# A four-stage transformer block with routed experts on one core: expert maps spread over the batches, loads and routed stage reordered

## The reference

```python
# 1 causal attention, 16 wide; the values are x itself
q = x @ w_q.T + b_q; k = x @ w_k.T + b_k
x = ln(x + softmax(mask(q @ k.T / 4)) @ x)
# 2 one linear map with ternary weights
x = ln(x + x @ (clip(round(w / s), -1, 1) * s).T)
# 3 q, k, v of x; a statistic of q and k per token, two small convolutions over the
#   tokens with a group norm (the ODE step), sigmoid, softmax over the 512 tokens;
#   v times that weight times a channel gate, then a projection
x = ln(x + (weights[..., None] * v * ch_w) @ proj_w + proj_b)
# 4 h = ln(x)*gamma+beta; a shared expert for all tokens and the best of 8 routed ones
out = silu(h @ sw1.T) @ sw2.T + p_top * (silu(h @ ew1[e].T) @ ew2[e].T)
x = ln(x + out)
```

## Time and profile before

| | us |
|---|---|
| median of 3 runs | 910.05 (909.46 to 910.09) |
| the profiled execution | 912.14 |
| its span, first to last instruction | 910.8 |
| TensorE busy | 782.4 (86%) |
| VectorE busy | 727.4 (80%) |
| ScalarE busy | 698.1 (77%) |
| GpSimd busy | 315.1 (35%) |

### The profile page before, as it was taken

One profiled execution on the slowest core, in us unless ns is written; L12 is line 12 of the kernel. 1 busy time (PEld: TensorE's weight loads), 2 busy tenths in 40 slices (PEclk: granted clock), 3 DMA queues, 4 the chain that ended last, 5 costly groups with the idle time before them and its releaser, 6 DMA issues. The chain is left out here.

```text
span 910.8 us, 18608 instructions
## 1 busy us (share of the span) xinstructions
PE 782.4 (86%) x5514; PEld 621.8 (68%) x5514; DVE 727.4 (80%) x2321; ACT 698.1 (77%) x1561; POOL 315.1 (35%) x384
## 2 busy tenths in 40 slices
PE   0568899999999999999999999988757878888783
PEld 0346678778878878878878877866435767767672
DVE  1777999778878878888887887977563889989995
ACT  0447887688697697697697797786746989999995
POOL 2000001012422323323333323434561555556556
PEclk9976999999999999999999999999887999999997
DMA  7132331110221211201203201101127775445441
GB/s 201 60 116 92 124 122 57 47 49 24 82 67 40 76 54 52 82 19 65 83 18 111 82 20 41 37 30 48 47 83 218 181 203 164 151 146 167 130 106 56
DMA packets 50979, 80.81 MB, mean 89 GB/s; under 512 B 8954, under 2 KB 27838, under 8 KB 50880
## 3 DMA queue, kind: packets, MB, share of 16 engines
q1 hardware_dynamic: 39056, 53.46, 20.7%
q0 software_dynamic: 9984, 25.29, 7.7%
q10 hardware_dynamic: 1840, 0.86, 0.3%
HBM read 49.57 MB, written 32.11 MB: 90 GB/s over the span
## 5 line engine op out<-in xcount | busy, mean ns | idle before, releaser
L3621 POOL DMA_INDIRECT out<-G_y,Gid x80 | 83.1, 1039 | 77.8 <-ACT G_y L1867 56.1
L1220 PE MATMUL bank<-E2T,G_Sh 128*128 (+1 forms) x320 | 74.3, 278 | 39.7 <-DVE G_Sl L3426 39.6
L3493 POOL DMA_INDIRECT rrec<-R,pos x64 | 64.3, 1005 | 82.0 <-DVE R L2111 67.2
L1849 ACT ACTIVATE G_S<-bank,e1b,e1s 128x256 f32<-128x256 f32 x160 | 91.6, 693 | 0.0
L519 PE MATMUL bank<-X,PT 128*128 128x257 f32 x320 | 82.5, 392 | 2.5 <-DVE X L1954 1.3
L3484 POOL DMA_INDIRECT hrec<-HN,pos x64 | 65.3, 1020 | 52.0 <-DVE pos L2234 37.2
L3452 POOL TENSOR_TENSOR R<-rstd,mhalf 128x4 f32<-128x4 f32 x16 | 17.4, 1089 | 184.2 <-DVE rstd L1910 184.2
L1208 PE MATMUL bank<-G_T,E1T 128*128 128x256 f16 x640 | 80.0, 280 | 1.0 <-DVE G_T L3417 1.0
L3460 POOL TENSOR_TENSOR R<-V,mhalf 128x8 f32<-128x8 f32 x16 | 26.7, 1666 | 142.7 <-DVE V L1920 142.7
L1220 PE MATMUL bank<-E2T,G_Sl 128*128 (+1 forms) x320 | 74.6, 278 | 0.0
L1208 PEld LDWEIGHTS bank<-G_T,E1T 128*128 (+1 forms) x640 | 64.4, 101 | 9.7 <-issue 1.4
(11 more groups left out here) (362 smaller groups left out, 2597.5 us busy)
## 6 DMA issues: line engine op xcount, KB each, us to landing
G_r<-rrec SPq DMA_DIRECT2D x40, 258.0 KB
G_h<-hrec SPq DMA_DIRECT2D x40, 257.0 KB, 2.8
X<-in_x SPq DMA_DIRECT2D x16, 512.0 KB, 5.2
XT<-in_xT SPq DMA_DIRECT2D x16, 512.0 KB, 4.3
e1n<-in_ew SPq DMA_DIRECT2D x8, 512.0 KB, 3.4
e2n<-in_ew SPq DMA_DIRECT2D x8, 512.0 KB, 3.4
rrec<-rpad SPq DMA_DIRECT2D x18, 129.0 KB, 4.9
hrec<-hpad SPq DMA_DIRECT2D x18, 128.5 KB, 4.7
```

What stands on the lines that cost most here:

```text
L1220: last = pe.matmul(banks[j][:, 0:D], x[w % NGB][:, f, j * P:(j + 1) * P], E2T[:, expert_of[w], f, :], start=k == 0, stop=k == 2 * FC - 1)
L1849: act.activation(G_S[w % 2][:, ff, :], bk[:, (ff - f0) * SLOT:(ff - f0 + 1) * SLOT], ACT.Silu, bias=e1b[:, expert_of[w], ff], scale=e1s[:, ...
L3493: pool.indirect_dma_start(rrec[:], bass.IndirectOffsetOnAxis(pos[b % 2][:, j:j + 1], 0), R[b % 2][:, j, :], None).then_inc(s[f"rrec{b % 2} ...
L3621: pool.indirect_dma_start(t["out"], bass.IndirectOffsetOnAxis(Gid[w % 6][:, j:j + 1], 0), G_y[w % 3][:, j, :], None, bounds_check=TOK - 1, ...
```

## The change

Shared and routed maps: the shared expert's map and the first routed one are made in the opening; the other seven come one per pair (`one0`, `one1`, `one_et0` and their like, map g+2 in pair g), in bank 2, between two ODE steps. The map buffers move: e1n, e2n and the clipped parts now share one place. `dg` is gone: `map_dg` multiplies a broadcast scale with the identity. `guard` runs twice, once for the shared expert, once for the routed ones, with a scale each. `rank` uses bank 6 in place of bank 2, and `up(b, 1)` waits for `place(b, 0)` in place of the first router step.

```diff
+        def load_e1(q):
+            if q == 1:
+                sp.wait_ge(s["et0"], 1)
+            elif q >= 2:
+                sp.wait_ge(s["et1"], q)
+                sp.wait_ge(s["dgm"], q)
+        def load_e2(q):
             if q >= 1:
+                sp.wait_ge(s["et0"], q + 1)
...
             pe.wait_ge(s["m0"], 7 * q + 5)
-            if q >= 1:
-                pe.wait_ge(s["e2s"], q)
-            b16 = banks[6][:].bitcast(F16)
+            if q == 1:
+                pe.wait_ge(s["e2s"], 1)
+            elif q >= 2:
+                pe.wait_ge(s["ode"], NO * (q - 1))
+            b16 = banks[6 if q < 2 else 2][:].bitcast(F16)
...
             if g >= 1:
-                pe.wait_ge(s["place"], at("place", GB * g - 1, 0))
+                pe.wait_ge(s["e2s"], g + 2)
...
             elif f == 1:
-                pe.wait_ge(s["rout"], at("rout", b, 0))
+                pe.wait_ge(s["place"], at("place", b, 0))
```

```diff
+        load_xT(0)
+        load_e1(0)
+        load_x(0)
+        load_e2(0)
+        load_xT(1)
+        load_small()
+        load_x(1)
+        load_e1(1)
+        load_tiny()
+        load_e2(1)
```

```diff
-            pe.matmul(bk[:, 0:w], KH[:, t], Qs[:, k * P:SEQ], start=True, stop=False)
-            pe.matmul(bk[:, 0:w], KL[:, t], Qs[:, k * P:SEQ], start=False, stop=False)
+            pe.matmul(bk[:, 0:w], Ks[:, t], Qs[:, k * P:SEQ], start=True, stop=False)
...
+            act.activation(Qs[64:128, :], banks[0][0:64, :], ACT.Identity, bias=bqk[0:64, :]).then_inc(s["qkhi"], 1)
```

```diff
-NGR, NGB = 4, 3
+NGR, NGB, NGS, NGY, NGI = 5, 4, 3, 4, 8
...
-            act.activation(G_Sh[w % NGB][:, f0:f0 + 2], G_S[w % 2][:, f0:f0 + 2], ACT.Copy, scale=sdn[:]).then_inc(s["gSh"], 1)
+            act.activation(G_Sh[w % NGB][:], G_S[w % NGS][:], ACT.Copy, scale=sdn[:, 1:2]).then_inc(s["gSh"], 1)
...
+            if j == 0:
+                if w < NF:
+                    expert_of[w] = bass.DynSlice(dve.value_load(q_exi[0:1, w:w + 1], min_val=0, max_val=NE - 1), 1)
...
-            dve.scalar_tensor_tensor(G_y[w % 3][:, j, :], banks[j][:, 0:D], G_r[w % NGR][:, j, D:D + 1], G_e2[w % 4],
+            dve.scalar_tensor_tensor(G_y[w % NGY][:, j, :], banks[j][:, 0:D], G_r[w % NGR][:, j, D:D + 1],
+                                     e2s[:, expert_of[w], :].rearrange("p o d -> p (o d)"),
```

More of the change, by code:

```diff
@@ L253, in program @@
     front_end = here[0]
-    here[0] = late_end
+    here[0] = front
     q_n = sb("q_n", [P, NE])
@@ L871, in pe_program @@
+        for i in range(4):
+            pv(1, i)
+        x2T(0, 0)
+        map_et1(1)
+        map_dg(1)
         x2T(0, 1)
-        map_dg(3)
         proj(2)
@@ L1115, in pe_program @@
-        rank(12)
+        hT(13, 0)
+        hT(13, 1)
+        guard_max(1)
+        for i in range(1, 4):
+            u(14, i)
+        logits(13)
         x2T(15, 0)
-        down(12, 0)
+        up(13, 0)
+        guard_bound(1)
+        rank(13)
         x2T(15, 1)
-        down(12, 1)
-        down(12, 2)
+        up(13, 1)
+        up(13, 2)
+        one_dg(7)
         gate1(15)
         dqk(15, 0)
-        down(12, 3)
         gate2(15)
-        dqk(15, 1)
-        hT(13, 0)
-        hT(13, 1)
@@ new lines, in act_program @@
+        gexp(1)
+        PS_(1)
+        one_r0(0)
+        x1c(2, 0)
+        Mh_(1)
+        for i in range(1, 4):
+            x1c(2, i)
+        qk(3)
+        T1h_(2, 0)
+        U_(1, 0)
+        U_(1, 1)
+        T1h_(2, 1)
+        U_(1, 2)
+        nmr_(3)
+        oexp(0)
+        U_(1, 3)
+        sq2(2, 0)
+        oexp2(0)
+        exp(3, 0)
+        sq2(2, 1)
+        exp(3, 1)
+        exp(3, 2)
+        sq2(2, 2)
+        exp(3, 3)
+        sq2(2, 3)
+        for i in range(4):
+            sq3(0, i)
@@ new lines, in dve_program @@
+        x2(1, 0)
+        chw(0, 3)
+        qklo(2)
+        qks(0, 3)
+        x2(1, 1)
+        x2(1, 2)
+        Ml_(0)
+        x2(1, 3)
+        max_(2, 0)
+        map0(1, 5)
+        ve0(1)
+        ve1(1)
+        max_(2, 1)
+        max_(2, 2)
+        guard(0, 0)
+        max_(2, 3)
+        x2p(0, 2)
+        map0(1, 6)
+        guard(0, 1)
+        one0(0, 0)
+        TTl_(1, 0)
+        one0(0, 1)
+        guard(0, 2)
+        TTl_(1, 1)
+        one0(0, 2)
+        rinv(2, 0)
+        x2p(0, 3)
@@ new lines, in dve_program @@
+        x2p(1, 0)
+        x1(2, 0)
+        rinv(2, 1)
+        x1(2, 1)
+        x2p(1, 1)
+        guard(0, 3)
+        qks(1, 0)
+        chw(1, 0)
+        bn0(2, 0)
+        chw(1, 1)
+        chw(1, 2)
+        rinv(2, 2)
+        chw(1, 3)
+        x1(2, 2)
+        bn0(2, 1)
+        qks(1, 1)
+        qks(1, 2)
+        one0(0, 3)
+        bn0(2, 2)
+        qks(1, 3)
+        guard(0, 4)
+        for i in range(3):
+            ode(0, i)
+        mv_(2, 0)
+        ode(0, 3)
+        ode(0, 4)
@@ new lines, in dve_program @@
+        ode(0, 18)
+        ode(0, 19)
+        max_(3, 3)
+        x2(2, 0)
+        guard(0, 7)
+        ode(0, 20)
+        ode(0, 21)
+        x2(2, 1)
+        ode(0, 22)
+        one0(0, 6)
+        ode(0, 23)
+        ode(0, 24)
+        x2(2, 2)
+        ode(0, 25)
+        ode(0, 26)
+        x3(0, 0)
+        x2(2, 3)
+        x3(0, 1)
+        x3(0, 2)
+        ve1(2)
+        rinv(3, 0)
+        x3(0, 3)
+        x1(3, 0)
+        guard(0, 8)
+        rinv(3, 1)
+        x2p(1, 3)
+        ve2(0)
@@ L3224, in dve_program @@
-        router(12, 6)
-        place(12, 0)
-        TTl_(15, 1)
-        x2p(15, 0)
-        ve2(13)
-        r(12, 0)
-        y(12, 1)
-        y(12, 2)
+        acc(12)
+        HTl_(13, 0)
+        HTl_(13, 1)
+        guard(1, 1)
+        guard(1, 2)
+        for i in range(3):
+            router(13, i)
+        rg(12)
+        for i in range(3, 6):
+            router(13, i)
+        TTl_(15, 0)
+        guard(1, 3)
+        place(13, 0)
+        x2p(15, 0)
+        Sl_(13, 0)
+        TTl_(15, 1)
```

2759 lines of the change are left out of this document (1284 added, 1475 removed), and 2 rows, old and new, of the table names.

## The result

The changed kernel takes **896.9 us** (median of 4 runs, 893.8 to 897.4) against 909.8 for the kernel before (909.2 to 910.1): ratio 0.985 [0.983, 0.988]. It is 12.9 us faster where 37 were forecast, and outside the range. Its profiled execution took 893.8 us (span 892.4), the fastest of its four, 18.3 less than the profiled one of before (912.1, span 910.8).

What follows compares the result with a forecast made beforehand. The prediction took TensorE's work to bound the loop over pairs, a dependent chain the drain, and mainly ScalarE the routed stage. Terms -12 - 8 + 5 - 8.5 + 1.5 - 15 = -37 gave 873 us, range 855 to 893.

Steps and rivals of the forecast that it cites:

- Load order, -12: Opening: issuing XT, X and the shared maps first starts attention earlier; -12 us, bounds -5 and -18.
- Maps leave the opening, -8: 44.6 to 157 us: seven maps fewer relieve VectorE and cut TensorE's idle and half-clock time; -8 us, bounds +3 and -20.
- One product, -8.5: Loop: transposed scores lose their second product, 0.60 us in each of some 14 batches; -8.5 us, bounds -7 and -10.
- Routed stage, -15: Routed stage: period falls from 5.11 to 4.70 us over 39 steps, fill +1; -15 us, bounds -3 and -19.
- Rival B: Routed stage keeps its period because VectorE is close behind ScalarE; -15 becomes -3, 885 us; chance 0.11.
- The drain, +1.5: Drain after the loop: later `up(b,1)`, eighth map and second guard cost little; +1.5 us, bounds -5 and +6.
- The same maps in the loop, +5: Loop: added VectorE and ScalarE work stays under TensorE, only waiting in order costs; +5 us, bounds 0 and +20.
- the loop's TensorE idle passes 20 us: Loop: sign that would show the prediction wrong, TensorE idle above 20 us.
- TensorE above 98% in the loop: Loop: sign expected if the maps term holds, TensorE busy above 98% beside VectorE at 90%.
- A: Loop slows: with VectorE at 91%, in-order queues leave TensorE waiting, +12 to +16 us; 887 us; chance 0.17.
- C: Loop: the map's chain stalls TensorE in every pair; slower from 5.3 us per map, 922 us at 7; chance 0.06.
- D: After the opening: the half-clock stretch vanishes, -10 us more; 863 us; chance 0.06.

Runs made afterwards that it cites:

- e8: e3 with the first XT, X and the shared expert's two tables loaded ahead of the small weights; 886.9 us.
- e3: The kernel before with two parts of the change, transposed scores as one product and the new routed stage, its front's order and maps untouched; 897.0 us.
- e12: e8 with VectorE's first list put in the order in which the loads land, all maps still in the opening; 883.7 us.
- e15: e13 with every piece of a map moved a few places later in the loop's lists; 899.4 us.
- e1: The kernel before with only the transposed scores as one product, including the third pass of q this needs; 904.1 us.
- e2: The kernel before with only the changed kernel's routed stage; 898.8 us.
- e9: The changed kernel with the loop's seven maps left out whole (set to zero at the start), the order of all else kept; 899.5 us.
- e13: e12 with seven maps moved from the opening into the loop, one per pair, the loop's lists otherwise in the old order; 930.7 us.
- e4: The changed kernel with the product of the transposed scores issued twice; 904.6 us.
- e5: The changed kernel with the loop maps' VectorE and ScalarE work cut to 16 columns for seven experts, TensorE transposing a constant; 936.4 us.
- e6: The changed kernel with only VectorE's work on the seven loop maps cut to 16 columns, TensorE transposing a constant; 926.5 us.

## Why the prediction was wrong, step by step

**Load order, -12: right, the exact figure in part by luck.** e8 shows 12.1, but its opening ran at a mean granted clock of 0.81 up to the projection of batch 4 and e3's at 0.88, so the two don't differ by the loads alone. In the changed kernel the first projection came at 7.83 (forecast 9) and the first reciprocal at 29.54 (32). On the way there VectorE's opening went otherwise than I had it:

```profile
14.29 1.22 DVE L2336 TENSOR_REDUCE esc<-e2n 128x2 f32<-128x1024 f32 x1 [1.33 <-DMA e2n<-in_sw]
...
17.17 0.69 DVE L2314 TENSOR_SCALAR e1n<-e1n 128x1024 f32<-128x1024 f32 x1 [1.59 <-ACT e1n L1461]
...
18.69 0.74 DVE L1942 SCALAR_TENSOR_TENSOR Qs<-bank,bqk,Qs 32x512 fp32r<-32x512 f32 x1
```

The second shared map was there at 14.3, not 19, since the first 20 us moved 265 GB/s and not 200. The Trainium skill's rule on queues taking turns (DMA: Bandwidth & Descriptors, "Queues, rings and completion order") is neither confirmed nor refuted: what VectorE needed from both queues had landed before the split of q and k could tell, and that split stood at 18.69 behind ScalarE's rounding.

**Maps leave the opening, -8: right in kind, too small.** e12 and e15 have the same loads first and differ in where the maps are: their projections of batch 4 stand 12.9 us apart (151.6 and 138.8), so -12.9, 1.8 us per map. The mean granted clock up to there is 0.85 and 0.84, so this comparison is an even one.

**One product, -8.5: the size was off, and -5.0 lies outside its bounds of -7 and -10.** e1's interval is -6.5 to -2.6. I multiplied the distance between two starts by the columns, 1.2 us per pair; the step became 1.0 shorter and its neighbours took part of that back, so the pair gained 0.68.

**Routed stage, -15: right.** -15.6 in the stage here, -14.2 in e2 (whose median moved by 10.3 only). The period is 4.71, with ScalarE at 174.6 and VectorE at 173.2 of 183.7, so both, not VectorE alone as I wrote, are nearly full. Rival B is refuted.

**The drain, +1.5: within its bounds.** The stretch from projection 14 to the first `gy` became 3.5 us shorter where 0 were forecast. It also holds one pair, so the drain by itself has no figure.

**The same maps in the loop, +5 (bounds 0 and +20): this is the step that failed.** The pair cost 5.9 us per pair against e1, about 33 over the loop. The step said: "Both stay under TensorE, so their work is covered; what is not covered is waiting in order", and behind it stood "only work taken off TensorE shortens it". I priced the waiting that the new order brings at 0.8 us per pair, from two places that I had looked at, and took the maps' own work on TensorE, 1.4 us per pair, as the same in the opening and in the loop. By e9 the order is the large part: without the maps the pair stays at 75.0.

Of the 5.9 us some 2.8 are idle time of TensorE (15.7 of 416 us in the loop) and 1.4 its own work on a map. The remaining 1.7 are spread over steps that take longer from start to start though no idle time stands in them: the block-3 statistics of q and k 12.3 for 11.6 us per pair, the transposes of `HN` 1.9 for 1.5, block 3's `u` 3.4 for 3.1. That this is waiting too is suggested, not shown, by the weight loads: per pair they are busy 54.8 us in e1 (190.8 / 240 x 69.0) and 56.2 after (180.3 / 240 x 74.8), longer by no more than the maps' own work. By that, some 4.5 of the 5.9 us are waiting, against the 0.8 of the step. In e9 the same sum is about 3 of idle time, no map work, about 1 for the clock and 2 for the longer steps: that its pair equals the changed kernel's is in part a coincidence, and does not show that the maps cost nothing there.

This agrees with a rule of the Trainium skill (Perfetto Trace Analysis, section "Identifying the Most-Contended Engine") that I did not weigh: the matmuls' busy share is a bad measure of how full TensorE is, and the weight loads' share a better one. It was 80% before, not 99.8. I had taken that a kernel whose TensorE is busy 99.8% of a stretch has slack everywhere else. It has none in its *order*: in the old one the view names no wait of TensorE in these 240 us, in the new one some come in every pair, though no engine's load explains it.

My sign for it, "the loop's TensorE idle passes 20 us", was a bad one: idle in 157 to 578 is 17.1 us, so it just didn't ring, at a loss of 28. The other one, "TensorE above 98% in the loop", did: it is at 96%.

**The rivals.** A (the loop slows, 887) had the right place and, at 4% of idle, about the right idle, but the wrong cause, VectorE's load (86%, not 91), and less than half the price. C (the map's chain stalls TensorE) is not seen in the changed kernel. e13 has C's price, 7.6 us per pair and slower than before, but not its mechanism: none of its four waits is on a map's clip. D came in part. In the changed kernel the half-clock stretch of the opening lasts 10.2 us in place of 27.3, with 6.4 us of TensorE's work in it in place of 20.5; by an estimate from these, 14.1 us of work that would take half, 7 of D's 10 us came, and they are part of the -28.4 of the opening:

```profile
40.00:60.00 20.00, 12.83 (x65) 9.55 (x66) 15.34 (x45) 13.22 (x29) 1.04 (x1) 0.74 0.25 80
...
43.40:53.60 10.20, 6.43 (x32) 4.43 (x30) 7.96 (x17) 6.23 (x11) 0.00 (x0) 0.50 0.12 24
```

D's reason, less idle time before, is not shown: e12, whose first projection also comes early (9.10), has a mean granted clock of 0.85 up to the projection of batch 4, where the kernel before has 0.91 and the changed one 0.96.

**Table loads.** 32 of them now, 14 fewer than 46, as counted, each 1283 ns as in the earlier trace rows; ScalarE's busy time fell by 17.5 us over the span, though other work on it changed too. The Trainium skill (ScalarE: Activation LUTs, "What ACT_TABLE_LOAD costs") adds a drain to each. Whether 18 or 37 us came free can't be told here, since ScalarE was not what bound the loop before.

**Do maps belong in the loop?** In the old order, not as tried: e15 against e12 saved 12.9 us in the opening and paid 16.0 in the five pairs and 13.8 behind them, 15.7 more in the median. Per pair a map cost 3.5 at best, of which 1.5 is TensorE's own work that it also has in the opening, beside idle time. In the new order they may pay by themselves: the pair has 74.8 us with a map, and by an estimate 74 to 74.2 without one (e9's 75.0 less the 0.8 to 1.0 of its clock), so a map costs under a microsecond there and saves 1.8 in the opening. What makes that a loss is the order around them, at 4 to 5 us per pair. Left open: whether there is an order that takes the maps and costs less; which part of the new one costs most; and why the changed kernel's median lies 3 us above its profiled execution.

## What to carry to other kernels

In a stretch where one engine is busy all the time, the order of its queue is itself a cost term: before pricing moved work, ask for each step of the new order whether its releaser is still done ahead of it, and give a rewritten order a wide price of its own. In this kernel's old order, work beside an idle engine in the opening was cheaper than the same work in the full loop, even where it looked as if it delayed the start. A test that leaves work out has to be read by stage, since leaving out can add something of its own elsewhere (here the zero filling). And take the parts that leave the order alone one by one: here they gave 25 us (e12), twice the whole change.

## What the runs showed of the hardware that was not expected

In a steady loop, TensorE's granted clock can fall to the 1.2 GHz level once or twice in each pair, for 3.4 to 6.8 us (e4, e5, e6), after the engine had been partly idle: in e6 busy 0.41 of 2 us, then 0.50; in e5 1.07 of 2, then 0.50 up to 382. The larger gap is not needed for it. e4 has before its stretch the same three waits as the changed kernel at the same place, 0.60, 0.20 and 0.93 us, and nearly the same busy time. Its clock fell, and the changed kernel's, which is the last line here, did not:

```profile
356.00:358.00 2.00, 1.07 (x22) 0.81 (x20) 1.96 (x5) 1.97 (x6) 0.00 (x0) 1.00 0.00 0
...
360.00:362.00 2.00, 2.00 (x6) 0.74 (x5) 1.10 (x6) 1.25 (x5) 0.00 (x0) 0.50 0.00 0
```

```profile
350.00:352.00 2.00, 1.23 (x23) 1.15 (x23) 1.74 (x7) 2.00 (x6) 0.00 (x0) 1.00 0.00 0
```

So the changed kernel's loop, at 1.00 all through, stood close to that fall, and what decides it is not shown by these runs. A gap can cost more than its length: in e5, which has less work on VectorE and ScalarE, the five pairs took 403.2 us in place of 375.6.

GpSimd's filling of a large tile with zeros (128x7168 fp16, 6.07 us) stretched VectorE's 128x128 cast beside it from 0.23 to 6.18 us (e9).
